# Self-attention scores masked on VectorE instead of by an identity matmul, and a new order of VectorE's work between the self projection and the next score phase

## The chip, the cores and the metric

One NeuronCore of a Trainium2 chip. TensorE (PE) multiplies, VectorE (DVE), ScalarE (ACT) and GpSimd (POOL) work on its results, and SyncE (SP) issues DMAs. The metric is the device time of one execution in microseconds, over several runs.

## The reference, cut to what matters

One post-norm decoder layer in fp32 for 16 independent batch elements of 256 tokens x 256 features, 16 heads of 16 features:

```
x = layernorm(x + self_attention(x))     # q, k: rms norm over a head, rotary embedding; causal mask
x = layernorm(x + cross_attention(x, ctx))                       # key mask and causal mask
x = layernorm(x + ffn(x))                # effectively light ffn + heavy ffn on every token (9 chunks of 128)
scores = where(causal, -inf, q @ k.T * scale); attn = softmax(scores)
```

## The kernel before, in words

The batch elements run as a software pipeline: step i handles the self attention of batch i (s), the cross attention of i-1 (c), the output of cross attention and the norm behind it of i-2 (f), the FFN of i-3 (l), and already projects q, k and v of batch i+2. A step has four phases on TensorE, each of 16 heads, and other matmuls are laid between the heads at places written out in tables at the end of the file (an entry `X_AT = n` puts the work X before head n):

- S1: the self scores of batch i, [query, key], whose row maxima VectorE takes. Between the heads: transposes of the first layer norm's output x1 (before head 1), the last group of cross values (3), the cross q projection (4), transposes and projection of the cross output (5, 9, 12), the nine FFN hidden chunks (6 and on).
- S2: the cross scores of batch i-1 and their maxima, with half of the FFN output.
- T1, T2: the same scores transposed, with the maxima subtracted by extra rows of the operands; ScalarE exponentiates, GpSimd zeroes what lies above the diagonal, and TensorE multiplies by the values. T2 also holds the self output (out_tokens, out_dims, out_proj at `OUT1_AT`) and the q, k, v projections of batch i+2 (`QK1_AT`, `V1_AT`).

Score tiles rotate through three PSUM banks; head h of a score phase may be written only when VectorE has taken the maximum of head h-3 (`wait_ring`). Every engine runs its own instruction list strictly in the order written; semaphores tie them together.

In both score phases TensorE first writes the causal bias (-1e30 above the diagonal) into the two diagonal blocks with an identity matmul (`idb`, `cmaskb`), and the two score matmuls accumulate onto it. VectorE then takes the three block maxima of a head with one `tensor_reduce` of 384 elements (L869), and `max_parts` joins two of them.

VectorE's order at the end of a step: split of the cross k (`split(2, s, 1, 0)`), the third layer norm (L946), the division of the self output (`normalise_heads(1, s)`, L906 and L909), `roots_qk(i + 2)` (sums of squares L971, then twelve dependent instructions, three for a first guess of 1/sqrt and three Newton steps of three), the self residual and its statistics (L918, L925 to L931), `scale_qk` for tile 0 (L996), the first layer norm, whose rstd GpSimd computes before its 14th mask of T2 (`RSTD1_AT` = 13, L1156), `scale_qk` for tile 1. Its output x1 is what TensorE transposes before head 1 of S1. GpSimd applies the rotary embedding of batch i+1 (`rotate`) at the head of step i; for batches 0 and 1 VectorE does it itself (`starting`). In S1 VectorE also splits the cross q before the maximum of head 5 (`SPLITQ_AT`, L853 to L858) and divides the cross output before head 7 (`NORM2_AT`), which the transposes `out_dims(2, f)` wait for.

## Time and profile before

| | us |
|---|---|
| median of three runs (lowest, highest) | 1112.89 (1111.15, 1113.44) |
| profiled execution, its own time | 1110.92 |
| its span | 1109.1 |
| PE busy in the span | 949.4 (86%) |
| DVE busy | 745.7 (67%) |
| ACT, POOL busy | 489.8, 456.8 |
| causal-bias matmuls on PE (512, both score phases) | 148.0, mean 289 ns of one |
| maxima on DVE (L869, 512) | 270.0, mean 553 ns of one |
| chain that ended last | PE 62%, DVE 16%, issue 13%, POOL 3%, ACT 3% |
| granted clock, mean | 0.936 |

A duration of a matmul is from its start until its last result is out; matmuls overlap, so the distance between two starts tells what one costs. The chain that ended last is followed back from the last instruction, at each step to what released it. The granted clock is TensorE's clock as a share of 2.4 GHz.

### The profile page before, as it was taken

Reading aid. Unit: us, or ns where it says so; the run is one execution under the profiler, and the core shown is the slowest. Engines: PE = TensorE matmul, PEld = TensorE weight load, DVE = VectorE, ACT = ScalarE, POOL = GpSimd, SP = SyncE. Lnnn points to the kernel's source line nnn. Section 1 sums busy time; section 2 is a strip of 40 time slices with the busy share of each in tenths; the row PEclk is TensorE's granted clock in tenths of the full one; section 3 lists DMA queues with packets and bytes.
Section 4 is the critical chain, followed back from the end, with each engine's and each line's share of the span. In section 5 each row is a group of like instructions: output and inputs, shape, how many; then the busy total and the mean of one; then the engine's idle time right before and its main releaser. Section 6 shows DMA issues by size and latency. Waiting matters only on the chain.

```text
span 1109.1 us, 21587 instructions
## 1 busy us (share of the span) xinstructions
PE 949.4 (86%) x7776; PEld 723.6 (65%) x7776; DVE 745.7 (67%) x1859; ACT 489.8 (44%) x1047; POOL 456.8 (41%) x867
## 2 busy tenths in 40 slices
PE   3465788899898989898998989898998989798886
PEld 2334465586767768686767767686867667675666
DVE  7737748677776877677767868677767868564522
ACT  1131252536454544546454544546454545444342
POOL 2025253535455463535454453535454453323130
PEclk8676899999999999999999989999999999998989
DMA  3537363634536162634555261634455270822300
GB/s 97 76 87 115 59 87 59 80 62 64 77 65 91 39 92 47 87 69 59 78 77 78 52 86 40 87 68 61 77 78 77 45 101 14 107 39 30 39 10 20
DMA packets 79642, 74.22 MB, mean 67 GB/s; under 512 B 8592, under 2 KB 78896, under 8 KB 79536
## 3 DMA queue, kind: packets, MB, share of 16 engines
q1 hardware_dynamic: 75872, 68.90, 41.2%
q10 hardware_dynamic: 3664, 3.94, 1.6%
q8 instruction: 62, 1.02, 0.5%
q14 instruction: 44, 0.36, 0.2%
HBM read 17.49 MB, written 4.20 MB: 20 GB/s over the span
## 4 chain that ended last, share of the span: by engine, by line
PE 62%; DVE 16%; issue 13%; POOL 3%; ACT 3%; DMA 2%; SPq 0%; ACTq 0%; POOLq 0%; DVEq 0%
PE bank L342 57%; PE bank L367 4%; DVE mx L869 4%; DVE x L946 2%; DVE rest L853 2%; POOL pr L1166 2%; ACT pr L728 1%; DVE on L909 1%; POOL rstd L1156 1%; DVE rden L906 1%; DMA stk2q<-nat2q 1%; DVE nat2q L856 1%; ACT nat2k L674 1%; ACT oT L674 1%; PE bank L495 1%
## 5 line engine op out<-in xcount | busy, mean ns | idle before, releaser
L869 DVE TENSOR_REDUCE mx<-bank 128x3 f32<-128x384 f32 x512 | 270.0, 553 | 129.9 <-PE bank L342 125.3
L728 ACT ACTIVATE pr<-bank 128x384 f32<-128x384 f32 x512 | 243.1, 499 | 236.0 <-PE bank L342 236.0
L1166 POOL TENSOR_SCALAR_AFFINE_SELECT pr<-pr 128x256 f32<-128x256 f32 x512 | 224.7, 448 | 239.3 <-ACT pr L728 238.1
L342 PE MATMUL bank<-cmaskb,idb 128*128 128x256 bf16 x512 | 148.0, 289 | 32.8 <-DVE mx L869 16.9
L342 PE MATMUL bank<-w,g 128*128 128x256 f32 x576 | 170.8, 389 | 1.1 <-ACT g L740 1.1
L1190 POOL TENSOR_TENSOR xTlow<-xT,xThigh 128x512 fp32r<-128x512 f32 x16 | 21.1, 1316 | 254.5 <-ACT xThigh L674 254.5
L740 ACT ACTIVATE g<-bank,b 128x256 f32<-128x256 f32 x144 | 68.2, 474 | 114.9 <-PE bank L342 114.4
L342 PEld LDWEIGHTS bank<-w,g 128*128 128x128 f32 x576 | 89.6, 190 | 5.2 <-ACT g L740 1.5
L342 PE MATMUL bank<-stk1k,stk1q 97*128 97x128 bf16 (+1 forms) x512 | 92.8, 267 | 0.0
L342 PEld LDWEIGHTS bank<-cmaskb,idb 128*128 128x128 bf16 x512 | 51.1, 100 | 59.4 <-DVE mx L869 29.0
L342 PE MATMUL bank<-stk1q,stk1k 100*128 100x256 bf16 (+1 forms) x512 | 80.3, 255 | 4.3 <-DMA stk1q<-mT 3.3
L342 PE MATMUL bank<-stk2k,stk2q 97*128 97x128 bf16 (+1 forms) x512 | 82.5, 247 | 0.0
L342 PE MATMUL bank<-stk2q,stk2k 100*128 100x256 bf16 (+1 forms) x512 | 73.3, 253 | 1.8 <-DMA stk2q<-mT 0.9
L1156 POOL TENSOR_TENSOR rstd<-ve,minus_half 128x2 f32<-128x2 f32 x48 | 33.3, 693 | 95.9 <-DVE ve L931 95.9
L342 PE MATMUL bank<-xnh,w1h 128*128 128x256 f32 x288 | 69.6, 323 | 2.3 <-DVE y L918 2.1
L342 PEld LDWEIGHTS bank<-stk1q,stk1k 100*128 100x128 bf16 x512 | 42.5, 100 | 38.4 <-ACT pr L728 8.9
L342 PE MATMUL bank<-pr,va 128*32 128x256 f32 (+1 forms) x1024 | 64.8, 379 | 2.4 <-POOL pr L1166 2.0
L342 PE MATMUL bank<-wo,onT 128*128 128x256 f32 x256 | 64.7, 397 | 1.8 <-ACT onT L674 1.8
L674 ACT ACTIVATE oT<-bank 128x256 f32<-128x256 f32 x128 | 50.0, 391 | 33.0 <-PE bank L342 26.6
L342 PEld LDWEIGHTS bank<-stk2k,stk2q 97*128 97x128 bf16 x512 | 50.5, 99 | 20.8
L342 PEld LDWEIGHTS bank<-stk1k,stk1q 97*128 97x128 bf16 x512 | 54.9, 107 | 11.1
L971 DVE TENSOR_REDUCE ss<-sq 128x32 f32<-128x512 f32 x32 | 21.8, 682 | 56.8 <-ACT sq L815 56.7
(143 smaller groups left out, 1835.6 us busy)
## 6 DMA issues: line engine op xcount, KB each, us to landing
stk1q<-nat1q SPq DMA_DIRECT2D x96, 128.0 KB, 4.7
stk1k<-nat1k SPq DMA_DIRECT2D x96, 128.0 KB, 6.5
stk2k<-nat2k SPq DMA_DIRECT2D x96, 128.0 KB, 4.6
stk2q<-nat2q SPq DMA_DIRECT2D x96, 128.0 KB, 4.7
xT<-in_xT SPq DMA_DIRECT2D x16, 256.0 KB, 2.8
x<-in_x SPq DMA_DIRECT2D x16, 256.0 KB, 5.2
ctxT<-in_ctxT SPq DMA_DIRECT2D x16, 256.0 KB, 3.0
out_x<-x SPq DMA_DIRECT2D x16, 256.0 KB, 5.2
```

The source lines that it names most:

```text
L342: return nc.tensor.matmul(out, lhsT, rhs, start=start, stop=stop, skip_group_check=check)
L367: last = nc.tensor.transpose(bank[k][:, c * T + t * P:c * T + (t + 1) * P], src[:, t, c * P:(c + 1) * P], idf[:, :])
L674: return nc.scalar.activation(out, in_, ACT.Copy)
L728: nc.scalar.activation(pr[:, h % (2 * HG), :], ring_bank("T", a, b, h)[:, 0:3 * P], ACT.Exp, scale=HD ** -0.5)\
L740: nc.scalar.activation(g[:, j, :], bank[HIDDEN_BANK[j % 2]][:, 0:T], ACT.Gelu, bias=b1[:, j:j + 1])\
L853: V.tensor_tensor(rest[:, :], bank[SPLIT_BANK[a][s]][:, :], n[:, 0, :], ALU.subtract)\
L869: V.tensor_reduce(mx3[:, h, :], scored[:, 0:3 * P].rearrange("p (k t) -> p k t", k=3), AX.X, ALU.max, negate=True).then_inc(s_mx[a], 1)
L946: V.tensor_scalar(xo[a][:, t, :], y[a][:, t, :], mv[a][:, t, 0:1], rstd[a][:, t:t + 1], ALU.subtract, ALU.mult).then_inc(s_x[a], 1)
L971: V.tensor_reduce(ss[:, t, :], sq[:, t, :].rearrange("p (h d) -> p h d", d=HD), AX.X, ALU.add)\
L1156: G.tensor_tensor(out, base, minus_half[:, 0:w], ALU.pow)\
L1166: G.affine_select(out=slot, in_=slot, compare_op=ALU.is_ge, fill=0.0, base=0, pattern=[[0, 2], [1, P]], channel_multiplier=-1).then_inc(s_ ...
L1190: G.tensor_tensor(xTp[1][:, :, :], xT[:, :, :], xTp[0][:, :, :].bitcast(f32), ALU.subtract)\
```

## The change: what it does

Five edits:

1. `MASKED_ON_PE` loses the self attention. In S1 TensorE leaves the identity matmul out. VectorE takes the maxima with two `tensor_tensor_reduce` a head, one of 128 elements (queries 0 to 127) and one of 256 (queries 128 to 255). Each adds the fp32 bias `cmask` from SBUF to the scores, writes the sum back over them in PSUM, and reduces with max into `mx2`. `max_parts(1)` has one instruction less. Cross attention stays as it was.
2. The three Newton steps leave `roots_qk` for a function of their own. The self residual and its statistics come right behind the first guess, then two Newton steps, the first layer norm, and the third Newton step.
3. `scale_qk` moves out of the end of the step into the next S1, before the maxima of heads 1 and 2 (`QN_AT`); the VectorE rotation of batch 0 moves with it, and the rotation of batch 1 goes to GpSimd.
4. `normalise_heads(1, s)` comes before `layer_norm(3, l)`.
5. Places: `out_dims(2, f)` one head later in S1 (9 to 10); in T2 `out_dims(1, s)` one head later (7 to 8), the second q, k projection (8 to 9), and ScalarE's copies and squares with them.

```
         def starting(b):
-            return isinstance(b, int) and 0 <= b < 2
+            return b == 0
...
-                for k in range(3):
...
+            def newton(b, k):
+                n = NEWTON * b + 3 * k
+                dve.wait_ge(s_new, n + 3)
+                V.tensor_tensor(nt[:, :, :], rr[:, :, :], rr[:, :, :], ALU.mult).then_inc(s_new, 1)
+                dve.wait_ge(s_new, n + 4)
+                V.scalar_tensor_tensor(out=nt[:, :, :], in0=ms[:, :, :], scalar=-0.5, in1=nt[:, :, :],
+                                       op0=ALU.mult, op1=ALU.mult).then_inc(s_new, 1)
+                dve.wait_ge(s_new, n + 5)
+                V.scalar_tensor_tensor(out=rr[:, :, :], in0=nt[:, :, :], scalar=1.5, in1=rr[:, :, :],
+                                       op0=ALU.add, op1=ALU.mult).then_inc(s_new, 1)
...
                 if live(s):
-                    maxima(1, s, {NORM2_AT: normalise_cross, SPLITQ_AT: split_cross_q})
+                    maxima(1, s, {QN_AT[0]: lambda: scaled(0), QN_AT[1]: lambda: scaled(1),
+                                  NORM2_AT: normalise_cross, SPLITQ_AT: split_cross_q})
                     max_parts(1, s)
                 else:
+                    scaled(0)
+                    scaled(1)
+                    split_cross_q()
                     normalise_cross()
-                    split_cross_q()
+                if starting(i + 1):
+                    rotate(dve, V, i + 1)
...
                     split(2, s, 1, 0)
+                if live(s):
+                    normalise_heads(1, s)
                 if live(l):
                     layer_norm(3, l)
-                if live(s):
-                    normalise_heads(1, s)
                 if live(i + 2):
                     roots_qk(i + 2)
                 if live(s):
...
                     add_residual(1, s, PROJ_BANK[1], x0)
                     statistics(1, s)
                 if live(i + 2):
-                    scale_qk(i + 2, 0)
+                    newton(i + 2, 0)
+                    newton(i + 2, 1)
                 if live(s):
                     layer_norm(1, s)
                 if live(i + 2):
-                    scale_qk(i + 2, 1)
-                if starting(i + 2):
-                    rotate(dve, V, i + 2)
+                    newton(i + 2, 2)
...
-MASKED_ON_PE = (1, 2)
+MASKED_ON_PE = (2,)
-X1T_AT, OUT2_AT, Q2_AT = 1, (3, 5, 9, 12), 4
+X1T_AT, OUT2_AT, Q2_AT = 1, (3, 5, 10, 12), 4
-K2_AT, OUT1_AT, QK1_AT, V1_AT = 1, (2, 4, 7, 10), (3, 8), 13
+K2_AT, OUT1_AT, QK1_AT, V1_AT = 1, (2, 4, 8, 10), (3, 9), 13
-COPY1_AT, SQ_AT = (0, 3, 4, 8), (5, 9)
-NORM2_AT, SPLITQ_AT, RESID2_AT, MAXT_AT, STAT2_AT = 7, 5, 1, 3, 6
+COPY1_AT, SQ_AT = (0, 3, 3, 9), (5, 10)
+QN_AT, NORM2_AT, SPLITQ_AT, RESID2_AT, MAXT_AT, STAT2_AT = (1, 2), 7, 5, 1, 3, 6
```

The branch of `maxima` that the self scores now take (it stood there unused):

```
for t, lo, hi in ((0, 0, P), (1, P, 3 * P)):
    masked = scored[:, lo:hi]
    last = V.tensor_tensor_reduce(out=masked, in0=masked, in1=cm[:, 2 * P - (hi - lo):2 * P],
                                  scale=1.0, scalar=-3e38, op0=ALU.add, op1=ALU.max,
                                  accum_out=mx2[:, t, h:h + 1])
last.then_inc(s_mx[a], 1)
```

## Rows read from the trace of the kernel before

**Rows 1.** The chain in order of time: start us, length us, engine, tile, line, count.

```profile
289.56 1.01 DVE mx L869 x2
...
965.46 1.02 DVE mx L869 x2
```

**Rows 2.** Waits of all engines: total us, times, longest us.

```profile
PE bank L367 <- DVE x L946: 32.5, 16, 2.5
```

**Rows 3.** Stretches: length, busy of PE, PEld, DVE, ACT, POOL, PEclk, DMA share, GB/s.

```profile
525.30:527.50 2.20, 0.00 (x0) 0.00 (x0) 1.96 (x8) 1.00 (x3) 1.64 (x4) 1.00 0.23 62
...
529.00:530.00 1.00, 1.00 (x8) 0.46 (x10) 0.80 (x2) 0.27 (x1) 1.00 (x3) 0.50 1.17 136
...
957.00:958.70 1.70, 0.95 (x17) 0.49 (x9) 0.87 (x3) 1.20 (x4) 1.70 (x5) 1.00 0.03 10
```

**Rows 4.** Timeline of DVE, end of T2: start us, length, line, operation, idle before.

```profile
513.33 0.82 DVE L946 TENSOR_SCALAR x<-y,mv,rstd 128x256 f32<-128x256 f32 x2
...
514.97 0.42 DVE L909 TENSOR_TENSOR on<-bank,rden 128x256 f32<-128x256 f32 x1
...
519.85 0.69 DVE L971 TENSOR_REDUCE ss<-sq 128x32 f32<-128x512 f32 x1 [3.87 <-ACT sq L815]
...
521.26 0.22 DVE L984 TENSOR_TENSOR nt<-rr 128x64 f32<-128x64 f32 x1
...
523.89 0.68 DVE L918 TENSOR_TENSOR y<-bank,x 128x512 f32<-128x512 f32 x1
...
525.61 0.17 DVE L931 TENSOR_SCALAR ve<-mv 128x2 f32<-128x2 f32 x1
...
526.59 0.88 DVE L946 TENSOR_SCALAR x<-y,mv,rstd 128x256 f32<-128x256 f32 x2 [0.21 <-POOL rstd L1156]
```

**Rows 5.** Timeline of PE, T2 and S1 of that step, and of the last batch.

```profile
515.45 0.66 PE L367 MATMUL bank<-idf,on 128*128 128x128 f32 x4 [0.88 <-DVE on L909]
516.03 0.86 PE L342 MATMUL bank<-pr,va 128*32 128x256 f32 x16
...
527.53 1.11 PE L367 MATMUL bank<-idf,x 128*128 128x128 f32 x4 [2.23 <-DVE x L946]
...
529.63 1.50 PE L342 MATMUL bank<-pr,va 128*32 128x256 f32 x16
...
538.27 0.66 PE L367 MATMUL bank<-idf,on 128*128 128x128 f32 x4 [0.60 <-DVE on L909]
...
540.75 0.28 PE L342 MATMUL bank<-cmaskb,idb 128*128 128x256 bf16 x1
540.87 0.33 PE L342 MATMUL bank<-stk1k,stk1q 97*128 97x128 bf16 x2
...
958.77 0.66 PE L367 MATMUL bank<-idf,x 128*128 128x128 f32 x4 [0.83 <-DVE x L946]
```

**Rows 6.** Timeline of POOL around the rstd of the first norm.

```profile
523.23 0.41 POOL L1166 TENSOR_SCALAR_AFFINE_SELECT pr<-pr 128x256 f32<-128x256 f32 x1 [0.19 <-ACT pr L728]
525.86 0.69 POOL L1156 TENSOR_TENSOR rstd<-ve,minus_half 128x2 f32<-128x2 f32 x1 [2.23 <-DVE ve L931]
```

**Rows 7.** Timeline of DVE in S1: split of the cross q, maxima, and behind the division.

```profile
534.03 0.68 DVE L853 TENSOR_TENSOR rest<-bank,nat2q 128x512 f32<-128x512 f32 x1
...
535.96 1.01 DVE L869 TENSOR_REDUCE mx<-bank 128x3 f32<-128x384 f32 x2
...
538.13 1.67 DVE L869 TENSOR_REDUCE mx<-bank 128x3 f32<-128x384 f32 x3
```

**Rows 8.** Groups of DVE by shape: busy us, mean ns of one, idle.

```profile
L250 DVE TENSOR_TENSOR sq<-qn,ropeS 128x128 f32<-128x128 f32 x16 | 3.9, 283 | 0.0
L246 DVE TENSOR_TENSOR qc<-qn,ropeC 128x256 f32<-128x256 f32 x8 | 3.3, 416 | 0.0
```

**Rows 9.** Timeline of DVE: two short instructions with no wait between them.

```profile
546.85 0.17 DVE L882 COPY nm<-mx 128x16 f32<-128x16 f32 x1
546.94 0.18 DVE L883 TENSOR_TENSOR nm<-mx 128x16 f32<-128x16 f32 x1
```

More of the change, by code:

```diff
@@ L981, in roots_qk @@
                                 ALU.mult, ALU.add).then_inc(s_new, 1)
-                for k in range(3):
-                    dve.wait_ge(s_new, n + 3 * k + 3)
-                    V.tensor_tensor(nt[:, :, :], rr[:, :, :], rr[:, :, :], ALU.mult).then_inc(s_new, 1)
-                    dve.wait_ge(s_new, n + 3 * k + 4)
-                    V.scalar_tensor_tensor(out=nt[:, :, :], in0=ms[:, :, :], scalar=-0.5, in1=nt[:, :, :],
-                                           op0=ALU.mult, op1=ALU.mult).then_inc(s_new, 1)
-                    dve.wait_ge(s_new, n + 3 * k + 5)
-                    V.scalar_tensor_tensor(out=rr[:, :, :], in0=nt[:, :, :], scalar=1.5, in1=rr[:, :, :],
-                                           op0=ALU.add, op1=ALU.mult).then_inc(s_new, 1)
+            def newton(b, k):
[8 more added lines that the diff above has]
+                                       op0=ALU.add, op1=ALU.mult).then_inc(s_new, 1)
             def scale_qk(b, t):
@@ L1027, in step, with scaled @@
                     scale_w1()
+                def scaled(t):
+                    if live(i + 1):
+                        scale_qk(i + 1, t)
                 def normalise_cross():
```

## The prediction

> **What bounds the kernel now.** I read the chain first, because the busy shares mix stages. It has a period: the same two maxima stand in it at 289.56 and, eleven steps on, at 965.46 [rows 1], so a step takes 675.9 / 11 = 61.45 us. Inside a step TensorE is the chain nearly everywhere and works without a gap, except where it waits for VectorE. The list of waits ranks these: 32.5 us in 16 waits for the first layer norm's output x1 [rows 2], then the waits for the divided outputs `on`. So a step gets shorter in three ways: less work for TensorE in gapless stretches, an earlier x1, an earlier `on`.
>
> The x1 wait costs more than its length. TensorE idles 2.23 us before 527.53 [rows 5], with full clock granted in that stretch; behind it the granted clock is 0.50 (1.2 GHz) from about 527.5 to 531 [rows 3]. The group of 16 value matmuls there takes 1.50 us against 0.86 [rows 5], 0.64 more; the transposes, 1.11 against 0.66, lose about 0.3 and two heads 0.25 each: 1.45 us a step. The last batch is a test that the trace makes itself: there are no Newton steps left in front of its residual, TensorE waits only 0.83 us [rows 5], and the granted clock stays 1.00 [rows 3].
>
> **T2, edits 2, 4 and 5.** I follow one step, 513 to 547, on its own clock.
> - `normalise_heads(1)` no longer stands behind two instructions of 0.82 us [rows 4]. Its input is there about 0.3 us later than VectorE would be, so `on` is complete near 514.93 instead of 515.39. In front of `out_dims(1)` TensorE now has a value group (0.79 from start to start) and a head (0.17). It reaches it at 515.5, and the 0.88 us gap [rows 5] is gone. The second q, k projection, the squares and the output projection, whose order is otherwise kept, come 0.6 to 0.9 earlier.
> - The second sum of squares moves from 519.85 to about 519.25. Between it and the residual stay 0.69 of its own and three short instructions (519.85 to 521.26 is 1.41 in all [rows 4]); the nine Newton instructions, 521.26 to 523.89 = 2.63 us, go behind. The projection is ready by 519.9. So the residual starts at 520.65 instead of 523.89, and `ve` (1.89 later, [rows 4]) is complete at 522.5 instead of 525.8.
> - GpSimd computes rstd only behind the mask of head 12. That mask ended at 523.64 [rows 6]; TensorE's heads 11 and 12 come 1.0 earlier, so 522.65. Then rstd 522.75 to 523.45.
> - VectorE, however, does two Newton steps first: 2 x 0.88 (a third of 2.63) from 522.45 to 524.2. The layer norm (0.88) ends at 525.05, transposes start at 525.15 instead of 527.53: 2.4 us earlier. What is late next is Newton itself, not rstd.
> - TensorE ends T2 at 523.77 instead of 524.85, does head 0, and waits 1.2 us. By the last batch I take the clock to stay at 1.00.
>
> **S1, edit 1: TensorE.** The bias matmul takes 0.12 us from its start to the next [rows 5]; without it a head is 0.17 instead of 0.28, 0.11 x 16 = 1.8 us a step where nothing else stops TensorE. The 148.0 us busy of all bias matmuls would mislead: these are overlapping durations.
>
> **S1, edit 1: VectorE.** A reduce of 384 elements takes 0.56 alone, but successors start 0.45 apart (1.01 for two, 1.67 for three [rows 7]). The trace has no fused multiply-reduce and no write into PSUM by VectorE. Per element, (416 - 283) / 128 = 1.04 ns [rows 8]. Lower bound of the pair: 384 x 1.04 = 0.40 plus twice the 0.05 that a reduce adds to its elements = 0.50. If nothing overlaps, the two rows themselves: 0.283 + 0.416 = 0.70. If operands come at half rate, 0.80 + 0.10 = 0.90, and I keep that as upper end. I take 0.63, between overlapped and not, since the nearest operation is that of [rows 8].
>
> The Trainium skill ("VectorE: DVE Perf Modes", section on the TRN2 errata) gives 120 + elements cycles at 0.96 GHz for sources in PSUM, an estimate of 0.65 for the pair. For the reduce it would say 0.525, where the trace has 0.45 between starts and 0.56 for one alone; the measurement decides, and the sum does without the rule.
>
> **S1 put together**, with P the price of the pair. VectorE ends the third Newton step at 525.85. Then head 0, scaling (0.61), head 1, scaling, heads 2, 3, 4, split (1.93), heads 5, 6, division (1.25; both from [rows 7]): the divided output is there at 525.85 + 7 P + 1.2 + 1.95 + 1.25 = 530.25 + 7 P, 534.7 for 0.63. TensorE reaches `out_dims(2)`, now before head 10, at 533.5 and waits for it to 534.85, where it waited 0.60 before head 9 [rows 5]. Banks do not hold it more: head 8 needs maximum 5 at 532.8, head 9 maximum 6 at 533.45. Behind it stand transposes, a hidden chunk and head 10 (1.5), then 6.2 us of gapless work (five hidden chunks of 0.72, five heads, the 1.72 projection). S1 ends at 542.5 instead of 546.75: 4.2 us, less 0.1 for the projection's wait on ScalarE. 4.1 a step; each 0.1 on P costs 0.7.
>
> Checks of what moves: q, k of batch i+1 are scaled 0.5 to 1.5 us relative to S1's start later, so GpSimd's rotation (9.6 us) ends near 537 while TensorE wants it near 542.5: hidden by 5 us; without that cover each us would count. `out_tokens(2)` needs the second scaling, 528.4, and comes at 528.9: bare. The stack DMAs of the cross q start with the split, at 529.7, and need about 8.5: ready at 538, before 542.5. The shorter `max_parts` is 0.1, at nothing.
>
> **Sum.** Newton stands in front of the residual for S1 of batches 3 to 14 in the steady state: 12 x 4.1 = 49. Batch 15 gains only the masks less a later `on`, 1.5. Batches 0 to 2: VectorE sets their pace, the masks cost it 16 x (0.63 - 0.46) = 2.7 each, against a rotation of 5 us off VectorE and the earlier x1 of batch 2; together 0, within 4. 1110.9 - 50.5 = 1060.4 for the profiled execution. It ran 2.0 below the median, so 1062.
>
> **Rivals.**
> - *The reduction is two instructions each.* Two short neighbours start 0.09 apart and last 0.18 [rows 9]: two more a head make P 0.50 + 0.18 = 0.68 at least and 0.90 at most. From about 0.85 VectorE's whole list (16 P + 4.45) also ends last. Gains 3.4 (at 0.73) to 1.9 us a step, and in batches 0 to 2, where I count half of the 48 heads, 2 to 6 us lost: 1074 to 1096. For it: a maximum must be written somewhere after the last element. Against: the reduce writes its three without any extra row. Chance 0.2. The skill's same page (section "Two Vector instructions with no wait between them") says that an op that also writes out its accumulator is two instructions, the main one and an accumulator read; by that rule, this case.
> - *The clock still falls* behind the remaining 1.2 us gap: 12 x 1.45 = 17 back, 1079. For it: the gap of 2.23. Against: 0.83 in the last batch. Chance 0.13.
> - *The reorder brings nothing*, because rstd or the output projection is late anyway, and only masks are saved: 12 x 1.5, 1095. Against: GpSimd stood idle 2.23 for `ve` [rows 6]. Chance 0.04.
> - *Slower: VectorE becomes the bound of S1.* Its list there is 525.85 + 16 P + 4.45; it reaches the old end, 546.75, at P = 1.03. If an add in place in PSUM with an extra operand costs 0.65 a piece, P = 1.3: 4.3 us a step lost (52) and 24 x 0.67 = 16 in batches 0 to 2: about 1180; at 1.1, 13 + 11, about 1137. For it: such a write is nowhere in the trace. Against: 1.03 is 2.7 ns an element, where the nearest operation has 1.04 [rows 8]. Chance 0.08.
>
> **How the numbers follow.** Forecast 0.55 (own range 1050 to 1072, P 0.52 to 0.75), rivals 0.2, 0.13, 0.04, 0.08. Range 1047 to 1095: below, P at its lower bound and some of the start gained; above, most of the first rival. A difference of 0.2%, 2.2 us, is about what a measurement can tell. Faster 0.90, same 0.02, slower 0.08.
>
> **What would show it.** No `idb` rows in S1, a head 0.89 apart beside a hidden chunk (1.00 before). The residual's start right behind the first guess; x1 wait near 1.2 with granted clock 1.00 behind it; the wait before `out_dims(1)` gone, the one before `out_dims(2)` near 1.3 and by VectorE. P is read from starts of consecutive pairs. Wrong if P is above 0.9, if half clock stands behind the x1 wait, or if the chain in S1 runs through the maxima beyond head 6.

## The result, and the profile after

1041.27 us, median of three runs (1036.35 to 1042.30), against 1112.89: the ratio is 0.935, interval 0.930 to 0.940. The forecast was 1062 in a range from 1047 to 1095, so the direction was right and the size was not: 71.6 us came where 50.9 were expected. Two of the ten executions of e17 below (1176 and 4802 us, at a mean granted clock of 0.79 and 0.17) are left out of its time, and the second of them is the one that was profiled. The profiled execution took 1041.27, its span 1039.5; PE is busy 907.4 us (87%), DVE 772.9 (74%), the mean granted clock is 0.946.

Two views say where VectorE's work went. First the groups by shape (busy us, mean ns of one, idle before them): each reduction is two instructions, the second of them a read of the accumulator in which the maximum was gathered.

```profile
L874 DVE CUSTOM_DVE_ANT_0 bank<-bank,cmask 128x256 f32<-128x256 f32 x256 | 118.9, 464 | 0.0
L874 DVE CUSTOM_DVE_ANT_0 bank<-bank,cmask 128x128 f32<-128x128 f32 x256 | 79.2, 309 | 39.2 <-PE bank L342 38.2
L874 DVE DVE_READ_ACCUMULATOR2_ANT mx<- 128x1 f32 x512 | 71.9, 141 | 0.0
```

Then the timeline of DVE at the end of T2 and in the first heads of S1 (start, length, line, operation); it answers to [rows 4, 7].

```profile
491.44 0.69 DVE L971 TENSOR_REDUCE ss<-sq 128x32 f32<-128x512 f32 x1 [2.03 <-ACT sq L815]
...
492.73 0.69 DVE L918 TENSOR_TENSOR y<-bank,x 128x512 f32<-128x512 f32 x1
...
494.46 0.17 DVE L931 TENSOR_SCALAR ve<-mv 128x2 f32<-128x2 f32 x1
...
496.23 0.84 DVE L946 TENSOR_SCALAR x<-y,mv,rstd 128x256 f32<-128x256 f32 x2
...
500.70 0.33 DVE L874 CUSTOM_DVE_ANT_0 bank<-bank,cmask 128x128 f32<-128x128 f32 x1
500.95 0.14 DVE L874 DVE_READ_ACCUMULATOR2_ANT mx<- 128x1 f32 x1
500.95 0.47 DVE L874 CUSTOM_DVE_ANT_0 bank<-bank,cmask 128x256 f32<-128x256 f32 x1
501.33 0.14 DVE L874 DVE_READ_ACCUMULATOR2_ANT mx<- 128x1 f32 x1
501.33 0.33 DVE L874 CUSTOM_DVE_ANT_0 bank<-bank,cmask 128x128 f32<-128x128 f32 x1
```

A pair's starts are 501.33 - 500.70 = 0.63 us apart. The read starts together with the instruction behind it, so its 0.14 us stand in the busy column beside that instruction's. Whether a pair would start earlier without the reads, no run shows. The residual starts 1.29 behind the second sum of squares, where it started 4.04 behind it [rows 4].

The timeline of PE of the same stretch, and of later steps (last bracket: idle before, and what ended it), answers to [rows 5].

```profile
485.18 1.04 PE L563 MATMUL bank<-idf,oT 128*128 128x128 f32 x8
...
487.94 0.66 PE L367 MATMUL bank<-idf,on 128*128 128x128 f32 x4
...
497.13 0.66 PE L367 MATMUL bank<-idf,x 128*128 128x128 f32 x4 [0.51 <-DVE x L946]
...
505.12 0.34 PE L342 MATMUL bank<-stk1k,stk1q 97*128 97x128 bf16 x2 [0.49 <-DVE mx L874]
505.75 0.34 PE L342 MATMUL bank<-stk1k,stk1q 97*128 97x128 bf16 x2 [0.29 <-DVE mx L874]
506.94 0.66 PE L367 MATMUL bank<-idf,on 128*128 128x128 f32 x4 [0.85 <-DVE on L909]
...
612.79 0.66 PE L367 MATMUL bank<-idf,x 128*128 128x128 f32 x4 [0.52 <-DVE x L946]
...
657.31 1.04 PE L563 MATMUL bank<-idf,oT 128*128 128x128 f32 x8
...
669.27 0.66 PE L367 MATMUL bank<-idf,x 128*128 128x128 f32 x4 [0.51 <-DVE x L946]
```

This step is 669.27 - 612.79 = 56.48 us. The wait for x1 fell from 2.23 to 0.51, and the one before `out_dims(1)` is gone (a value group behind it now waits 0.23 for GpSimd). The rest stands in front of `out_dims(2)`: 0.49 + 0.29 + 0.85 = 1.63, all by VectorE. The first line is the one I had not looked for: the transposes of the self output (`oT`) start without a wait. In the kernel before, the same eight transposes waited for ScalarE's copy:

```profile
700.68 1.09 PE L563 MATMUL bank<-idf,oT 128*128 128x128 f32 x8 [0.86 <-ACT oT L674]
```

The chain that ended last (start, length, what) stays on VectorE for 15 us of this step, from the sum of squares at 491.44 to the end of the division at 506.9. In S1 it runs through scalings, maxima and the split:

```profile
500.85 0.19 DVE bank L874
501.04 0.06 DVE mx L874
501.09 0.06 DVE bank L874
...
502.11 0.56 DVE rest L853
...
505.31 0.32 DVE bank L874
505.63 0.06 DVE mx L874
505.69 0.12 DVE rden L906
```

Stretches of after (length, then busy of PE, PEld, DVE, ACT, POOL, granted clock, DMA share, GB/s), against [rows 3]: behind the x1 wait the clock stays at 1.00 (2.4 GHz). But behind `out_dims(2)` it is 0.50 (1.2 GHz) in this step. I call such a stretch of 3 to 4 us a spell. There is one in 5 of the 12 steps from 3 to 14; the third stretch, a whole step long and without a spell, ran at 1.00.

```profile
497.00:507.00 10.00, 8.23 (x73) 6.62 (x74) 9.79 (x42) 5.03 (x9) 8.26 (x15) 1.00 0.84 121
...
508.50:510.50 2.00, 2.00 (x12) 1.91 (x10) 1.03 (x6) 1.28 (x3) 1.56 (x2) 0.50 1.14 137
...
635.00:690.00 55.00, 52.40 (x463) 40.47 (x462) 45.37 (x156) 30.41 (x65) 29.51 (x55) 1.00 0.55 79
```

A spell costs its step 1.35 us: steps with one take 57.82, steps without one 56.47. I call the latter a clean step.

The spans, 1109.1 and 1039.5, cut at the bias matmul of head 4 in S2, 2.8 to 2.9 us behind the first matmul of S2. Where I write below that S2 of a step begins, this mark is meant:

| part of the span | before | after | gain | forecast |
|---|---|---|---|---|
| up to S2 of step 3 | 241.6 | 232.6 | 9.0 | 4.1 |
| 11 steps, to S2 of step 14 | 680.4 | 627.9 | 52.5 | 45.1 |
| last step, to S2 of step 15 | 57.1 | 55.1 | 2.0 | 1.5 |
| tail, from there to the end | 130.0 | 123.8 | 6.1 | 0 |

### The profile page after: what moved, and what is told of

The parts are those of the page before. It is cut to its first block, busy times and chain, and to the rows that moved or that the text cites. A ratio compares the mean times of both kernels' runs of the same rounds, so it can differ in the third digit from the quotient of the medians.

```text
span 1039.5 us, 21827 instructions
## 1 busy us (share of the span) xinstructions
PE 907.4 (87%) x7520; PEld 688.1 (66%) x7520; DVE 772.9 (74%) x2595; ACT 489.2 (47%) x1047; POOL 463.9 (45%) x883
## 4 chain that ended last, share of the span: by engine, by line
PE 50%; DVE 25%; issue 10%; POOL 4%; DMA 3%; ACT 3%; SPq 1%; ACTq 1%; POOLq 0%; DVEq 0%
PE bank L342 47%; DVE bank L874 5%; DVE mx L869 3%; POOL pr L1176 2%; PE bank L367 2%; DMA y<-in_b 2%; ACT pr L728 2%; DVE x L946 1%; DVE mx L874 1%; DVE y L918 1%; DVE qn L998 1%; DVE st L925 1%; DMA stk2q<-nat2q 1%; DVE nt L988 1%; DVE rest L853 1%
## 5 line engine op out<-in xcount | busy, mean ns | idle before, releaser
L874 DVE CUSTOM_DVE_ANT_0 bank<-bank,cmask 128x128 f32<-128x128 f32 (+1 forms) x512 | 168.3, 387 | 39.2 <-PE bank L342 38.2
L869 DVE TENSOR_REDUCE mx<-bank 128x3 f32<-128x384 f32 x256 | 133.5, 552 | 27.5 <-PE bank L342 24.4
L342 PE MATMUL bank<-stk1k,stk1q 97*128 97x128 bf16 (+1 forms) x512 | 90.0, 269 | 40.8 <-DVE mx L874 25.2
L342 PEld LDWEIGHTS bank<-stk1k,stk1q 97*128 97x128 bf16 x512 | 37.8, 103 | 69.5 <-DVE mx L874 42.1
L342 PE MATMUL bank<-cmaskb,idb 128*128 128x256 bf16 x256 | 71.0, 277 | 5.1 <-DVE mx L869 2.2
L246 POOL TENSOR_TENSOR qc<-qn,ropeC 128x256 f32<-128x256 f32 x60 | 49.4, 823 | 51.7 <-DVE qn L998 33.9
L874 DVE DVE_READ_ACCUMULATOR2_ANT mx<- 128x1 f32 x512 | 71.9, 141 | 0.0
L342 PE MATMUL bank<-wo,onT 128*128 128x256 f32 x256 | 67.2, 408 | 2.6 <-ACT onT L674 2.5
L342 PE MATMUL bank<-pr,va 128*32 128x256 f32 (+1 forms) x1024 | 56.3, 338 | 5.2 <-POOL pr L1176 5.2
```

The source lines that it names most:

```text
L246: ops.tensor_tensor(qc[:, t, s * D:(s + 1) * D].rearrange("p (h d) -> p h d", d=HD), qn[:, t, s * D:(s + 1) * D].rearrange("p (h d) -> p h ...
L342: return nc.tensor.matmul(out, lhsT, rhs, start=start, stop=stop, skip_group_check=check)
L869: V.tensor_reduce(mx3[:, h, :], scored[:, 0:3 * P].rearrange("p (k t) -> p k t", k=3), AX.X, ALU.max, negate=True).then_inc(s_mx[a], 1)
L874: last = V.tensor_tensor_reduce(out=masked, in0=masked, in1=cm[:, 2 * P - (hi - lo):2 * P], scale=1.0, scalar=-3e38, op0=ALU.add, op1=ALU.max,
```

## The experiments

Each is told as a time, and a ratio to the kernel before on the same chip with its interval. "x1 wait" is TensorE's before the transposes of x1. Spells are counted over the steps 3 to 14, and read, like all parts of a span, from the one profiled execution of each kernel.

**First round: the parts, and the clock.** Theory: the x1 wait, with the half clock behind it, is the large term, and the masks help a little. Rival: the masks on VectorE cost as much as they bring.

*e1: all but edit 1.*

```
-MASKED_ON_PE = (2,)            # against after
+MASKED_ON_PE = (1, 2)
```

> The changed kernel, but the self scores masked by the identity matmul and reduced by one tensor_reduce as before (edits 2 to 5 alone). Theory (the early x1 carries most): the x1 wait stays short and the clock behind it high, VectorE's maxima are 0.17 us a head cheaper, so the divided cross output comes earlier; TensorE pays 16 x 0.11 = 1.8 us again. Step 57.5 to 58.5 us, about 1055 us in all, some 80% of the gain. Rival (the masks carry most, since TensorE is the bound): step above 60, over 1085 us.

1030.4 us, 0.925 (0.921 to 0.928): faster than the change as it was made, whose interval it does not touch. The expectation, 1055, missed by 25 us. Every step takes 56.4 without a spell, where after has clean steps of 56.47 and five spells; S2 of step 3 begins at 225.1 instead of 232.6. So in this setting edit 1 loses 11 us, but next to nothing in a clean step: between the two profiled executions, which are 14 us apart, 7.6 lie at the start and 6.7 are the five spells. One step of it (timeline of PE):

```profile
655.91 0.65 PE L367 MATMUL bank<-idf,x 128*128 128x128 f32 x4 [0.40 <-DVE x L946]
...
665.32 0.66 PE L367 MATMUL bank<-idf,on 128*128 128x128 f32 x4 [0.61 <-DVE on L909]
```

*e2: edit 1 alone.*

```
-MASKED_ON_PE = (1, 2)          # against before
+MASKED_ON_PE = (2,)
```

> The kernel before with edit 1 alone (self masks on VectorE). Theory: TensorE saves 0.11 a head, but heads 0 to 8 save it into the waits for x1 and for the divided cross output, and the maxima of heads 5 and 6 come 0.36 later; net about 0.5 to 1 us a step, 1095 to 1105 us. Rival (edit 1 carries most): 1.8 us or more a step, 1080 us or less. Second rival (VectorE becomes the bound): above 1113 us.

1110.9, 0.9985 (0.996 to 1.001): nothing. A step takes 61.47 where it took 61.60. TensorE's saved 1.8 us a step turn into waits, here 0.15 + 1.48 where the kernel before had 0.60:

```profile
600.04 0.34 PE L342 MATMUL bank<-stk1k,stk1q 97*128 97x128 bf16 x2 [0.15 <-DVE mx L874]
601.86 0.66 PE L367 MATMUL bank<-idf,on 128*128 128x128 f32 x4 [1.48 <-DVE on L909]
```

*e3: after, with all Newton steps in front of the residual again.*

```
+                    for k in range(3): newton(i + 2, k)     # behind roots_qk(i + 2)
...
-                    newton(i + 2, 0); newton(i + 2, 1)      # in front of layer_norm(1, s)
-                    newton(i + 2, 2)                        # behind it
```

> The changed kernel with all three Newton steps back in front of the self residual, all else as changed. Theory: x1 comes about 1.7 us later, TensorE idles about 2.5 us before its transposes, the half clock stands behind that wait again in every step (1.3 to 1.5 us): step near 59.5 to 60, 1070 to 1080 us. Rival (Newton in front costs nothing that the later waits would not give back): step below 58, under 1050 us.

1068.9, 0.961 (0.956 to 0.966): 27.6 us slower than after. The x1 wait is 2.33 again, in every step. The half clock is not: it stands behind only 4 of 12 such waits (in three of these steps a second spell follows some 10 us later, behind `out_dims(2)`). Timeline of PE, then stretches right behind two equal waits, the first at 624.07:

```profile
624.07 0.66 PE L367 MATMUL bank<-idf,x 128*128 128x128 f32 x4 [2.33 <-DVE x L946]
...
685.09 0.66 PE L367 MATMUL bank<-idf,x 128*128 128x128 f32 x4 [2.33 <-DVE x L946]
```

```profile
624.10:627.60 3.50, 3.50 (x30) 2.54 (x31) 3.50 (x18) 0.98 (x2) 2.49 (x6) 0.71 1.07 142
685.10:688.60 3.50, 3.50 (x34) 2.75 (x35) 3.50 (x18) 0.98 (x2) 2.49 (x6) 1.00 1.07 143
```

This was the first crack in my account of the clock.

*e4: after, with the split of the cross q behind the division.*

```
-QN_AT, NORM2_AT, SPLITQ_AT, ... = (1, 2), 7, 5, ...
+QN_AT, NORM2_AT, SPLITQ_AT, ... = (1, 2), 7, 9, ...
```

> The changed kernel with the split of the cross q on VectorE before the maximum of head 9 instead of 5, so behind the division of the cross output. Theory (what ends last in S1 is the divided output): the waits before heads 8 and 9 and before out_dims (0.49, 0.29, 0.85 us) and the half clock behind them go: step 54.5 to 55.5 us, 1015 to 1025 us. Rival (the split then holds the score banks, or the cross stack's DMAs come too late for S2): a new wait of 1 us or more before head 11 or before S2, 1037 us or more.

1013.9, 0.910 (0.907 to 0.914). The 1.93 us of the split leave the chain in front of the division. Behind x1's transposes S1 keeps a wait of 0.19, a clean step is 54.9, and there is no spell in the steps 3 to 14. A new wait, 0.94 for the stack DMA that the later split feeds, appears in one of the eleven steps, this one:

```profile
442.43 0.34 PE L342 MATMUL bank<-stk1k,stk1q 97*128 97x128 bf16 x2 [0.19 <-DVE mx L874]
447.10 0.28 PE L342 MATMUL bank<-cmaskb,idb 128*128 128x256 bf16 x1 [0.94 <-DMA stk2q<-nat2q]
```

**Second round: is it the clock, and whose are the 20 us?**

*e5: before, with TensorE kept busy in the x1 wait.* The 13 transposes write what the next ones overwrite.

```
+                pe.wait_ge(s_y[1], b + 1)
+                for _ in range(13):
+                    nc.tensor.transpose(bank[X1T_BANK][:, 0:P], idf[:, :], idf[:, :])
```

> The kernel before, with 13 transposes of the identity (about 1.9 us of work whose result is overwritten) written into TensorE's wait for x1 of each batch, so that it isn't idle there. The order of everything else and the time of x1 stay. Theory (the half clock behind that wait costs 1.3 to 1.5 us a step in the kernel before): the spells go, step 60.0 instead of 61.46 us, 1090 to 1097 us. Rival (the spell comes anyway, or what follows waits for VectorE and not for TensorE): above 1108 us. A filler that ends after x1 would cost up to 0.3 us a step.

1093.4, 0.982 (0.976 to 0.987). The data come no earlier, and the clock behind the wait is 1.00 in the stretch below, where before has 0.51 in the 3.5 us behind its wait (715.30 to 718.80). A step takes 60.1 instead of 61.6, 20 us in all: 1.5 a step, the prediction's 1.45.

```profile
640.40:643.90 3.50, 3.50 (x36) 2.75 (x37) 2.47 (x5) 0.98 (x2) 3.42 (x8) 1.00 1.09 140
```

*e6: after without edits 4 and 5* (the division behind the third norm, places 9, 7, 8 and the copies at 4 and 8).

```
-X1T_AT, OUT2_AT, Q2_AT = 1, (3, 5, 10, 12), 4
+X1T_AT, OUT2_AT, Q2_AT = 1, (3, 5, 9, 12), 4
-K2_AT, OUT1_AT, QK1_AT, V1_AT = 1, (2, 4, 8, 10), (3, 9), 13
+K2_AT, OUT1_AT, QK1_AT, V1_AT = 1, (2, 4, 7, 10), (3, 8), 13
-COPY1_AT, SQ_AT = (0, 3, 3, 9), (5, 10)
+COPY1_AT, SQ_AT = (0, 3, 4, 8), (5, 9)
```

> The changed kernel without edits 4 and 5 (third layer norm in front of the self division again, out_dims, second projection, squares and copies at their old heads). Theory: the wait before out_dims(1) comes back at 0.9 us a step, and the one before out_dims(2) sits before head 9 instead of 10 and grows by about 0.9 (a hidden chunk less in front is none; it only moves): step 57.8 to 58.5, 1052 to 1062 us. Rival (they only shift waits): within 3 us of the changed kernel, 1041.

1061.7, 0.954 (0.948 to 0.960), 20 us slower than after. A clean step is 58.1, 1.6 more than after's, and there is one spell instead of five, so the price of taking these edits out is partly hidden. The waits of one step: 0.86 for ScalarE's copy `oT`, 0.88 before `out_dims(1)`, 1.48 before `out_dims(2)`.

```profile
608.14 1.09 PE L563 MATMUL bank<-idf,oT 128*128 128x128 f32 x8 [0.86 <-ACT oT L674]
610.61 0.66 PE L367 MATMUL bank<-idf,on 128*128 128x128 f32 x4 [0.88 <-DVE on L909]
620.57 0.66 PE L367 MATMUL bank<-idf,x 128*128 128x128 f32 x4 [0.23 <-DVE x L946]
```

*e7: after without edit 3* (the rotation of batch 1 is back on VectorE with it).

```
-                    maxima(1, s, {QN_AT[0]: lambda: scaled(0), QN_AT[1]: lambda: scaled(1), ...})
+                    maxima(1, s, {NORM2_AT: normalise_cross, SPLITQ_AT: split_cross_q})
...
+                    scale_qk(i + 2, 0); scale_qk(i + 2, 1)  # behind newton(i + 2, 2)
```

> The changed kernel without edit 3: both scalings of q, k at the end of VectorE's step, behind the third Newton step, and the rotation of batches 0 and 1 on VectorE. Theory: in the steady state the same 1.2 us of VectorE's work stands in front of the same maxima, only the maximum of head 0 comes later, which nobody waits for: same step within 0.3 us; the start gains or loses up to 5 us (the rotation of batch 1, 5 us of VectorE, against that of GpSimd, 9.6 us): 1036 to 1046 us. Rival (head 3 waits for the maximum of head 0): 0.5 us or more a step, above 1047 us.

1046.5, 0.941 (0.935 to 0.947), where after has 0.935: 5 us, and the two intervals overlap. The mean step is as long as after's (57.1), as the theory had it, but only because e7 has no spell. Its clean step is 57.07 against 56.47, for what the rival said: a head near the start of S1 waits for a maximum that now comes later. So edit 3 is worth 0.6 in a clean step, and the five spells of after hide it. S2 of step 3 begins 2.9 later.

```profile
616.59 0.34 PE L342 MATMUL bank<-stk1k,stk1q 97*128 97x128 bf16 x2 [0.93 <-DVE mx L874]
```

*e8: e1 with the split behind the division.*

```
-MASKED_ON_PE = (2,)          ... SPLITQ_AT = 5
+MASKED_ON_PE = (1, 2)        ... SPLITQ_AT = 8
```

> Edits 2 to 5, the self masks back on TensorE, and the split of the cross q before the maximum of head 8 instead of 5. Theory (VectorE's extra work on the masks is worth more than TensorE's matmul wherever a VectorE result ends last): the wait before out_dims(2), 0.6 us a step with the reordering alone, goes, the start keeps its 7.6 us: step 55.5 to 56.0, 1018 to 1024 us. Rival (with the late split TensorE is the bound of S1, and 16 bias matmuls cost 1.8 us a step again): step above 56.4, above 1028 us.

1030.4, 0.925 (0.920 to 0.930), as e1: my expectation fell, and e4, with the masks on VectorE, is 16 us faster. Not all of that is the masks, for e4 has the split one maximum later, and here head 11 waits:

```profile
613.57 0.28 PE L342 MATMUL bank<-cmaskb,idb 128*128 128x256 bf16 x1 [0.61 <-DVE mx L869]
```

With this wait taken off, its step of 56.3 would be 55.7 against e4's 55.0; neither has a spell. So 0.7 a step gained by edit 1 once the split is out of the way is my estimate; the like kernel with the split at 9 was not run.

**Third round: mixtures, and the places alone.**

*e9 and e10: masks of batches 0 to 2 on TensorE, the others on VectorE*, with `SPLITQ_AT` 8 and 5.

```
+        def on_tensor(a, b):
+            return a in MASKED_ON_PE or b < PE_UNTIL
+PE_UNTIL = 3
```

> The changed kernel with the split of the cross q before head 8, and the self scores of batches 0 to 2 (where no FFN work stands between the heads and VectorE sets the pace) masked by TensorE, those of batches 3 to 15 by VectorE. Theory: the start is that of the reordering alone (S2 of step 3 begins near 225 us, 4 us earlier than with masks on VectorE throughout and the late split), and the step is 54.5 to 55.0, because the split one head earlier takes 0.6 of the 0.94 us wait for the cross stack's DMA: 1004 to 1010 us. Rival (head 11 waits 0.6 us or more for the maximum behind the split, as it does with masks on TensorE): step 55.3 or more, 1012 us or more.

1026.4, 0.923 (0.919 to 0.928). Missed by 16 us: the rival came. It is only 4 us from e8, with overlapping intervals. With the split before maximum 8 the wait in front of head 11 is 0.90 to 1.54, where e4, with 9, has none there and 0.19 in front of head 12; the tail is 129.0 against 124.2.

> The changed kernel with the masks of batches 0 to 2 alone back on TensorE. Theory (VectorE is the bound of the first batches, and the masks cost 7 to 8 us there): 1032 to 1036 us, S2 of step 3 begins near 225 us instead of 232.6, the steps stay at 56.5 or 57.8. Rival (the start is bound by loads and code, not by the masks): within 2 us of the changed kernel, 1041.

1040.1, 0.935 (0.931 to 0.939): no different from after. S2 of step 3 begins 2.7 earlier, and then 7 of the steps have a half-clock spell instead of 5. It masks batches 0 to 2 as e1 does, yet is 4.9 behind e1 at this mark, and 2.7 behind it already in the first step's S2, where both have run the same masks. Up to the mark the mean granted clock (from 18 us, where the matmuls begin) is 0.80 in e10 as in after, and 0.83 in e1. So at the start the masks cost 2.7 us between two kernels of the same clock; the other 4.9 of e1's lead go with the clock, which I argue and did not test.

*e11: the cross masks on VectorE too.*

```
-MASKED_ON_PE = (2,)
+MASKED_ON_PE = ()
```

> The changed kernel with the cross scores masked on VectorE too. In S2 TensorE needs 0.71 us a head with the bias matmul and would need 0.60; VectorE needs 0.63 for the pair, and four other pieces of its work stand in S2. Theory: VectorE becomes the bound of S2, 16 x 0.63 + 2.9 of other work = 13 against 12.1 on TensorE: 1 to 2 us a step lost, 1060 to 1075 us. Rival (TensorE is the bound everywhere but for a few waits): 1 to 1.8 us a step gained, 1015 to 1025 us.

1054.9, 0.948 (0.944 to 0.953), 14 us slower than after. Three waits like those of S1 now stand in S2 too (0.63, 0.29, 0.29; here the first). They cost little themselves, for a clean step is 56.66 against 56.47, but there are spells in 10 of 12 steps instead of 5:

```profile
639.50 0.34 PE L342 MATMUL bank<-stk2k,stk2q 97*128 97x128 bf16 x2 [0.63 <-DVE mx L874]
```

*e12: edits 4 and 5 alone* (e6's places the other way, on the kernel before).

```
+                if live(s): normalise_heads(1, s)      # now in front of layer_norm(3, l)
-COPY1_AT, SQ_AT = (0, 3, 4, 8), (5, 9)
+COPY1_AT, SQ_AT = (0, 3, 3, 9), (5, 10)                # and OUT2_AT, OUT1_AT, QK1_AT as in after
```

> The kernel before with edits 4 and 5 alone. Theory: the wait before out_dims(1) (0.9 us a step) goes, but the projection and with it the residual come 0.6 earlier only in front of Newton steps that do not move, so x1 comes at most 0.6 earlier: 0.6 to 0.9 us a step, 1100 to 1106 us; in the tail of the last batch, without Newton steps, the wait before out_dims(1) of 1.66 us falls under 0.6, and the 11 us of half clock behind it go, so the last stretch (from S2 of step 15) is 125 instead of 130 us. Rival (the half clock in the tail has nothing to do with that wait): last stretch 129 us or more.

1056.0, 0.951 (0.946 to 0.956): 55 us from two edits that I had valued at 0.6 to 0.9 a step, and the largest miss of the study. TensorE still waits 2.23 for x1, but the clock behind it is 1.00 in all steady steps (timeline, then the stretch behind):

```profile
618.63 0.66 PE L367 MATMUL bank<-idf,x 128*128 128x128 f32 x4 [2.23 <-DVE x L946]
```

```profile
618.70:622.20 3.50, 3.50 (x36) 2.75 (x37) 2.48 (x5) 0.98 (x2) 3.42 (x8) 1.00 1.10 140
```

A step went from 61.60 to 58.05, 3.55 us: 0.86 (copy), 0.88 (`out_dims(1)`), 0.20 (`out_dims(2)`, 0.60 to 0.40) and 1.5 for the clock (e5) make 3.4. The start gained 9.3 and the tail 4.2; that tail (125.8) is near the expected 125, but see on the tail below.

**Fourth round: are the clock's us the same in all of them?**

*e13: e12 with e5's filler.*

```
+                pe.wait_ge(s_y[1], b + 1)
+                for _ in range(13):
+                    nc.tensor.transpose(bank[X1T_BANK][:, 0:P], idf[:, :], idf[:, :])
```

> Edits 4 and 5 alone (1056 us, x1 wait 2.2 us a step, granted clock 1.00 in the steady state), with the same 13 transposes in the wait for x1 that took 20 us off the kernel before. Theory (the filler was worth only the half clock that it took away; the wait itself is not on TensorE's side): no spell to take away here, so 1054 to 1058 us. Rival (the filler helps in another way, or the idle time itself costs): 1040 us or less.

1055.2, 0.950 (0.947 to 0.953), as e12. Where there is no spell the filler brings nothing, although it shortens the x1 wait from 2.23 to 0.80 as in e5. So its 20 us in e5 were the clock's.

*e14: edit 2 alone* (the scaling of tile 0, which stood in front of the first layer norm, goes behind the third Newton step with it).

```
-                    scale_qk(i + 2, 0)                      # behind statistics(1, s)
+                    newton(i + 2, 0); newton(i + 2, 1)
...
+                    newton(i + 2, 2); scale_qk(i + 2, 0)    # behind layer_norm(1, s)
```

> The kernel before with edit 2 alone (self residual in front of the Newton steps, the scalings behind the third). Theory: the residual starts 2.6 us earlier, x1 1.6 to 1.7 us earlier, since GpSimd's rstd is not earlier than the 13th mask and two Newton steps stand before the norm: 1.6 us a step, and if the half clock goes with the shorter wait 1.4 more: 1065 to 1070 us. Rival (the spell of half clock stays, as the x1 wait isn't what makes it): 1085 to 1090 us.

1073.2, 0.965 (0.962 to 0.968): 37 us. A clean step is 58.87, and 2 of 12 steps have a spell. The waits that take the place of x1's 2.23 are these two:

```profile
627.57 0.28 PE L342 MATMUL bank<-cmaskb,idb 128*128 128x256 bf16 x1 [0.52 <-DVE mx L869]
...
635.17 0.66 PE L367 MATMUL bank<-idf,on 128*128 128x128 f32 x4 [1.00 <-DVE on L909]
```

*e15: edit 4 alone.*

```
+                if live(s): normalise_heads(1, s)      # in front of layer_norm(3, l)
```

> The kernel before with edit 4 alone (self division in front of the third layer norm, all places as before). Theory: the divided self output comes 0.46 us earlier and TensorE's wait before out_dims(1) falls from 0.88 to 0.4, which shifts everything behind by 0.45: 1105 us if the half clock stays in every step, 1083 if it goes. Rival (edit 5's places are what matters, the head and the value group in front of out_dims): 1110 us or more.

1094.4, 0.987 (0.982 to 0.991), 11 us below the expectation. The wait before `out_dims(1)` is 0.50 instead of 0.88 and a step with a spell 61.22 instead of 61.60, as expected; the spells stay in 11 of 12 steps. What I had not expected is the rest: 3.4 at the start, and a tail that is 5 us shorter.

*e16: e4 with the masks of batches 0 to 2 on TensorE and only one Newton step before the layer norm.*

```
-                    newton(i + 2, 1)                   # moved behind layer_norm(1, s)
...
+PE_UNTIL = 3
+QN_AT, NORM2_AT, SPLITQ_AT, ... = (1, 2), 7, 9, ...
```

> The late split (before head 9) with masks on VectorE from batch 3 on, and one Newton step instead of two in front of the first layer norm. Theory: in the run with the late split (1014 us) rstd was ready 0.5 us before the second Newton step ended, so x1 comes 0.5 earlier and the x1 wait of 0.51 goes; the wait for the cross stack's DMA (0.94) grows with it unless the split starts earlier too, which it does by the same 0.3 to 0.5: step 54.6, start 3 us less: 1004 to 1010 us. Rival (the DMA wait takes all of it): step 55.0, 1010 to 1013 us.

1010.6 (1008.3 to 1011.2), 0.909 (0.906 to 0.912): faster than both kernels, though its interval overlaps e4's; it lies in the range of the rival and 0.6 above that of the theory. The x1 wait is down to 0.22, a new wait of 0.27 stands behind it, a step takes 54.7:

```profile
701.43 0.66 PE L370 MATMUL bank<-idf,x 128*128 128x128 f32 x4 [0.22 <-DVE x L949]
703.60 0.34 PE L345 MATMUL bank<-stk1k,stk1q 97*128 97x128 bf16 x2 [0.27 <-DVE mx L877]
```

**Fifth round: the one number that I had passed over,** ScalarE's copy `oT` for `out_tokens(1)`, before head 4 or before head 3.

*e17: that number alone, on the kernel before.*

```
-COPY1_AT, SQ_AT = (0, 3, 4, 8), (5, 9)
+COPY1_AT, SQ_AT = (0, 3, 3, 8), (5, 9)
```

> The kernel before with one number of edit 5 alone: ScalarE copies the last group of the self output before the exponential of head 3 instead of head 4. Theory (the prediction passed over this one): TensorE waits 0.86 us a step for that copy before out_tokens(1), 14.8 us in all, and the wait goes: 0.8 us a step where nothing else ends last, 1096 to 1101 us if the half clock stays in every step, 1076 to 1080 if it goes with the shift. Rival (the copy's wait only moves into the wait for the divided output behind it): 1108 us or more.

1112.4, ratio 1.001 (0.9985 to 1.004): nothing. The rival came.

*e18: after, with that number back.*

```
-COPY1_AT, SQ_AT = (0, 3, 3, 9), (5, 10)
+COPY1_AT, SQ_AT = (0, 3, 4, 9), (5, 10)
```

> The changed kernel with that one number put back (head 4). Theory: the 0.86 us wait before out_tokens(1) returns in each step and x1, which hangs on the self projection, comes as much later: 0.8 us a step and 2 to 3 us at the start and the end, 1052 to 1057 us, less up to 7 if the half clock behind out_dims(2) goes. Rival: within 2 us of the changed kernel, 1041.

1051.2, 0.9475 (0.943 to 0.952) where after has 0.935 (0.930 to 0.940): 10 us. A clean step is 57.15 against 56.47, 0.68 a step or 7.5 over eleven, and 7 steps have a spell instead of 5, 2.7 more. The wait is back as it was:

```profile
605.43 1.09 PE L563 MATMUL bank<-idf,oT 128*128 128x128 f32 x8 [0.85 <-ACT oT L674]
607.91 0.61 PE L367 MATMUL bank<-idf,on 128*128 128x128 f32 x4
617.07 0.66 PE L367 MATMUL bank<-idf,x 128*128 128x128 f32 x4 [0.52 <-DVE x L946]
```

## Why the prediction was right or wrong

**T2: right, and one wait missed.** A usual step of before, with its spell, and a clean one of after are 61.60 and 56.47. From the `oT` transposes to those of x1 it was 14.55 (before, 715.23 - 700.68) and is 11.96 (669.27 - 657.31): 2.59, forecast 2.4. The x1 wait is 0.51 where 1.2 was forecast, so I had TensorE too early there; counted from the `oT` transposes, x1, which sets the end, came when worked out. GpSimd's rstd (495.03) was not the late one; the two Newton steps were, as said.

The step that failed is the list of what edit 5 does in T2. I took the places one by one and valued only `out_dims(1)`; the earlier copy went in at nothing, without a reason. It moved one head ahead of the transposes that need it, and these now start 23.97 us behind the mark in S2 where they started at 24.99, with a wait of 0.86 gone. e18 gives the price in the changed kernel: 0.68 in a clean step, since T2 gives a part of the gain back (the transposes of x1 start 11.96 us behind those of `oT` in after, 11.64 in e18). e17 shows that by itself the copy is worth nothing. The reason may be that in the kernel before an earlier TensorE would only come sooner to `on`, which VectorE completes when it does; this is argued from the 0.88 wait behind it, for e17 has no profile of an ordinary execution. Which of the other edits it needs beside it was not tested.

**S1: right to 0.2.** P is 0.63, the value taken. `out_dims(2)` starts 9.81 us behind x1's transposes (679.08 against 669.27 in the step without a spell gives the same), forecast 9.7. Its wait is 1.63 in three pieces, forecast 1.3 in one; the banks did hold TensorE a little, at two heads (0.50 and 0.29), which I had ruled out. From the transposes of x1 to the mark in S2 it gained 1.52, forecast 1.7. So 1.02 + 2.59 + 1.52 = 5.13 a step against 4.1. Of the 1.03 between them the copy is 0.68, two thirds. The rest, 0.35, lies in T2, which gained more than worked out even without the copy (e18: 11.64 from the `oT` transposes to those of x1, so 2.91 where I had 2.4); what it is made of stays open.

**Reductions of two instructions: true, and cheaper than I had it.** The first rival's premise holds, and the Trainium skill says it ("VectorE: DVE Perf Modes", section "Two Vector instructions with no wait between them": an accumulator output adds a read). This trace agrees, with 512 such reads of 141 ns. But a read starts with the operation behind it, and the pair stays at 0.63 where the rival had 0.68 to 0.90. That it is just the value taken is partly luck: 0.63 was chosen between two bounds, not derived. The 0.45 between the starts of two reduces rests on the pair in [rows 7] alone; the three of that row, 1.67 in all, are 0.56 apart.

**The clock: the price right, the cause wrong.** I read 1.45 us a step for the half clock (e5: 1.5, 20 us in all) and laid it to the length of the x1 wait. e12 keeps 2.23 and has no spell in the steps 3 to 14, e3 has 2.33 in every step and a spell behind it in 4 of 12, and after has spells behind `out_dims(2)` that came with waits of only 1.63, the same as in its clean steps. So the wait's length does not settle it. (The test of the last batch that I leaned on was thin too: the row cited ends before its transposes; behind them, 958.80 to 962.00, the clock is 1.00 as I said.) For after, the gain came as forecast; 5 spells of 1.35 took 6.7 back. What decides where a spell falls stays open.

It also makes comparisons misleading, because two kernels may differ by spells alone. Times of steps without spells separate the two:

| kernel | clean step, us | steps with a spell, of 12 | tail, us | mean granted clock in the tail |
|---|---|---|---|---|
| before | none (61.60 with) | 12 | 130.0 | 0.92 |
| e5, filler | 60.1 | 0 | 130.3 | 0.92 |
| e14, edit 2 | 58.87 | 2 | 129.7 | 0.92 |
| e12, edits 4 and 5 | 58.05 | 0 | 125.8 | 0.94 |
| e3, Newton first | 58.23 | 4 | 129.0 | 0.92 |
| e6, without 4 and 5 | 58.11 | 1 | 125.9 | 0.95 |
| e18, without the copy | 57.15 | 7 | 123.8 | 0.96 |
| e7, without edit 3 | 57.07 | 0 | 124.7 | 0.96 |
| e11, all masks on VectorE | 56.66 | 10 | 126.0 | 0.94 |
| after | 56.47 | 5 | 123.8 | 0.96 |
| e1, without edit 1 | 56.42 | 0 | 124.2 | 0.97 |

And e12 and e14 each collect most of the clock's 20 us, so their gains (55 and 37) are together more than the 83 of both with edit 3 (e1).

**The other terms that were mis-sized.** Eleven steps: 11 x 5.13 = 56.4, plus 2.8, nearly all of it one step of before whose spell was twice as long (the clock is 0.50 from about 650 to 657) and which took 64.3, less 6.7 = 52.5, forecast 45.1. Without the spells of after, which nobody foresaw there, the forecast would have been further off. The start: forecast 0 for batches 0 to 2 as 8.1 lost to masks against as much gained. By e10 the masks cost 2.7 and not 8.1, so the reorder earned 11.7, near the 12.2 that I had for it (8.1 and batch 3's 4.1), and the 4.9 that came on top at the start are the masks, which I had priced too high. By e1 the masks would cost 7.6 and the reorder have earned 16.5; but its clock up to the mark was another. The tail: forecast nothing, gained 6.1. By the table this is the clock again: at a mean of 0.92 the tail takes 129.0 to 130.3, at 0.96 or 0.97 it takes 123.8 to 124.7, and e3, whose Newton steps stand only in earlier steps, so that its tail is after's instruction for instruction, takes 129.0. So the 6.1 cannot be credited to an edit, and why the clock of the tail differs stays open. I had not looked at this stretch of before, the longest of its low stretches there (after's, 985 to 992.5, is 7.5 long, at 0.55):

```profile
1005.00:1016.00 11.00, 8.98 (x53) 5.42 (x54) 2.91 (x9) 3.41 (x9) 2.77 (x7) 0.53 0.01 1
```

**What I called a gain and is none here.** By the prediction edit 1 was worth 1.5 to 1.8 a step. A clean step of after is 56.47, that of e1, without the edit, 56.42. In S1 of after VectorE is the chain up to the division, so its dearer maxima, seven pairs in front of it at 0.17 more each, take back what TensorE saves; with the split behind the division (e4 against e8) the edit does gain. The prediction's own sum had the late divided output in it, and with its own numbers for the masks left on TensorE (`out_dims(2)` at about 534.5 instead of 534.85, then six heads at 0.11 more) the edit would have come out at 0.3 a step, but I did not ask. The rest of e1's lead of 11 us is the five spells, whose cause is open, and the start. The sign of being wrong that I named, a chain through the maxima beyond head 6, did not come: behind the division the chain is TensorE's.

## What to carry to other kernels

Value every number of a placement table by the instruction that waits for it, and walk the PE waits of one whole period, small ones too: 0.86 us in a line that the argument did not touch was worth 0.68 a step, 7.5 us of the 10 that its removal cost. Before moving work from the busiest engine to another, ask which of them ends last at the next joint; here edit 1 took 1.8 us a step off TensorE and gained nothing. An edit measured alone can collect a shared gain such as the clock's, so test it by taking it out of the full change as well as by putting it into the old kernel, and compare steps with the same granted clock before you price an edit by the whole time.

## What the runs showed of the hardware

- A multiply-reduce of fp32 with one source in PSUM, the other in SBUF, and the result written back to PSUM took 309 ns for 128 elements and 464 ns for 256 (means, after). Back to back the two start 0.25 and 0.38 us apart, accumulator reads included.
- Waits of TensorE of the same length, 2.23 to 2.33 us, were followed by half clock in every step, in 4 of 12, or in none, in three kernels with nearly the same work around them (before, e3, e12). Filling the wait with transposes took the half clock away where there was one (20 us of 1113), and did nothing where there was none.
- The last 124 to 130 us of the kernel, the same work in nearly all runs, took 129.0 to 130.3 us where the mean granted clock was 0.92 (before, e3, e5, e9, e14) and 123.7 to 125.1 where it was 0.96 or 0.97 (after, e1, e4, e7, e8, e10, e15, e18).
